# Attention values of the last steps on one Trainium2 core: two split bursts of groups 28 and 30 placed as one burst each

## The chip, the cores and the metric

The kernel runs on one core of a Trainium2 chip. The metric is the device time of one execution in microseconds (us); less is better. The kernel before takes 639.27 us, the median of three runs (638.93 to 641.06).

## The reference

For eight sequences of 512 tokens with 512 features, attention with 16 heads of 32 features is added to the input. A conditioning row is projected too and added to queries and keys, not to values.

```python
Q = split(x @ Wq.T + bq); K = split(x @ Wk.T + bk); V = split(x @ Wv.T + bv)
cQ = Q + split(tokens @ Wq.T + bq); cK = K + split(tokens @ Wk.T + bk)
scores = einsum('bhqd,bhkd->bhqk', cQ, cK) / sqrt(32)
out = einsum('bhqk,bhkd->bhqd', softmax(scores), V)
x = x + merge(out)
```

## The kernel before, in words

The work is cut into 32 groups (`G` = 8 sequences times 4 sets of four heads). A group needs, in this order: its projections; 16 *maxima* matmuls (line 429), each followed by a VectorE reduction of its bank to row maxima (line 751); 16 *scores* matmuls (line 447), each followed by a ScalarE exponential out of the bank into SBUF (line 647); three GpSimd additions over the four key chunks (line 959), for the softmax sums; the *values* matmuls (line 467), four key chunks of four heads, one head in each quarter of the output bank; the *totals* (line 475), small matmuls that finish the sums; and on VectorE the inverse of the sums, its turn, the product and the addition of bias and input (lines 784, 800, 807, 821). A matmul of values is shown as two records in the trace, so a chunk of four matmuls is "x8" there and "x4" in the program's order.

TensorE's order is written by hand. Step t has 16 slots; slot n issues scores n of group t, then as many maxima of the group ahead and projection matmuls as tables say (`MAXIMA`, `LATE_PROJ`), and at chosen slots a burst of values of group t-1. In step 29 (i = 0) and 30 (i = 1) maxima of groups 30 and 31 run; step 31 (i = 2) has only scores. The projections end in slot 3 of step 29. `END_VALUES_AT` says at which slots of the last three steps the bursts stand.

What waits for what near the change:

- A maxima matmul uses one of two banks and waits for the reduction two before it (`maxima`, wait on `v_mx`).
- A scores matmul waits for the exponential that last used its bank. There are two such banks up to slot 6 of step 29, three from slot 7 on (`END_BANKS`), and four from slot 12 of step 30 on. The fourth was a maxima bank, so scores of slot 12 of step 30 wait for all reductions of maxima (`scores`, wait on `v_mx` for `SLOTS * G`).
- A burst of values waits for its exponentials (`a_e`), and for the finished group that used its output bank (`v_f`).
- `end_totals(g)` waits for the key sums of g on VectorE (`v_s`), and for the inverse of group g-1 (`v_f`).
- The first GpSimd addition of group 29 waits for the exponentials of slots 4 to 7 of step 29 (`add`, `a_e`). GpSimd then makes five additions in a row, three for group 29 and two for group 30, and `last_sums(30)` on TensorE waits for the last (`p_a`), behind the first half of the values of group 31 in slot 11 of step 31.
- The maxima rows of group 31 go to SBUF by four small DMAs after the last reduction (line 1037), and scores of slot 0 of step 31 wait for them (`d_mr`).

The bank of a scores matmul follows from this piece, the oldest of the n banks that are open:

```python
n = 2
for i, slot, banks in END_BANKS:
    if u >= SLOTS * (G - 4 + i) + slot:
        n = banks
i = min(range(n), key=lambda i: last_use[i])
```

Of the kernel before, what the change touches and what calls it, by code (L numbers as in the profile page):

```python
# [14 lines left out]
KC = D // P  # L15
G = B * KC
# [52 lines left out]
LATE_LO = ((5, 13), (16, 24), (32, 34), (40, 47))  # L69
LATE_V = (50, 57, 67, 69)  # L70

END_VALUES_AT = ((5, 13), (15,), (3, 7))
END_TURN_AT = 5
END_SUMS_AT = 11
POOL_ADDS = 2
# [5 lines left out]
def cond_attention(nc, xT, condT, wqT, wkT, wvT, biasT, outT):  # L81
    with ExitStack() as ctx:  # L82
# [146 lines left out]
        for u in range(SLOTS * G):  # L229
# [5 lines that stand above are left out]
# [8 lines left out]
        def o_bank(g):  # L243
            return {G - 3: other_bank(), G - 2: OB[1], G - 1: OB[0]}[g] if g >= G - 3 else OB[g % 2]
# [34 lines left out]
        def maxima_at(t, n):  # L279

            return FIRST_MAXIMA[n] if t == 0 else 1 if t < G - EARLY else MAXIMA[t - (G - EARLY)][n] if t < G - 1 else 0

        def exponentials(g):
            return Pt2 if g in (G - 3, G - 1) else Pt
# [13 lines left out]
        def st_unit(g, kc, j):  # L298
            return SLOTS * g + 4 * kc + j + 1

        def finished(g, i):
            return FIN * g + i
# [17 lines left out]
        def tensor_program(e):  # L320
# [61 lines left out]
            def condition_sum(bk):  # L382
                e.wait_ge(p_sel, 5)
                e.wait_ge(a_tc, 1)
                for c in range(KC):
                    for j in range(4):
                        m = e.matmul(bk[32 * j:32 * j + 32, 32 + c * B:32 + (c + 1) * B],
                                     rr[:, c * P + 32 * j:c * P + 32 * j + 32], sel[:, 0:B], start=True, stop=True)
                m.then_inc(t_vb, 1)
# [17 lines left out]
            def project(kind, g, n):  # L407
                if kind == "v":
                    project_v(g, n)
                else:  # L410
                    project_qk("qk".index(kind), g, n)

            def maxima(u, total=None):
                g, m = divmod(u, SLOTS)
                qc, j = divmod(m, 4)
                q, k = stacked(0, g), stacked(1, g)
                if u >= 2:
                    e.wait_ge(v_mx, u - 1)
                if total is not None:
                    e.wait_ge(v_f, finished(total, 1))  # L420
                if m == 0:
                    stack_landed(e, 0, g)
                    stack_landed(e, 1, g)
                    if g < NSLOT:
                        e.wait_ge(p_ks, g + 1)
                        e.wait_ge(v_z, g + 1)
                    if g == G - 4:
                        e.wait_ge(d_ks, 48)
                e.matmul(MXB[u % 2][:, :], q[:, j, qc * P:(qc + 1) * P], k[:, j, :],  # L429
                         start=True, stop=True).then_inc(t_mx, 1)  # L430

            def scores(g, n):
                kc, j = divmod(n, 4)
                q, k = stacked(0, g), stacked(1, g)
                if n == 0:
                    e.wait_ge(d_mr[g % 2], 64 * (g // 2 + 1))
                u = SLOTS * g + n
                if st_bank_before[u] >= 0:
                    e.wait_ge(a_e, st_bank_before[u] + 1)
                elif u < 2:  # L440

                    e.wait_ge(v_lo, 3 + u)
                elif st_bank_of[u] == 2:
                    e.wait_ge(a_v, G)
                else:
                    e.wait_ge(v_mx, SLOTS * G)
                e.matmul(st_bank(u)[:, :], k[:, j, kc * P:(kc + 1) * P], q[:, j, :],  # L447
                         start=True, stop=True).then_inc(t_st, 1)

            def values(g, chunks):  # L450
                b, c = divmod(g, KC)
                if 0 in chunks:
                    if g == G - 3:
                        e.wait_ge(v_ml, 1)
                    elif g >= G - 2:
                        e.wait_ge(v_f, finished(g - 3, FIN))
                    elif g >= 2:
                        e.wait_ge(v_f, finished(g - 2, FIN))
                if g == 1 and 0 in chunks:
                    e.wait_ge(v_vb, 1)  # L460
                for kc in chunks:
                    if c == 0:
                        e.wait_ge(a_v, KC * b + kc + 1)
                    e.wait_ge(a_e, st_unit(g, kc, 3))
                    for j in range(4):
                        h = 4 * c + j
                        m = e.matmul(o_bank(g)[32 * j:32 * j + 32, :], V[:, b % 2, kc, h * HD:(h + 1) * HD],  # L467
                                     exponentials(g)[:, kc, j, :], start=(kc == 0), stop=(kc == KC - 1))
                    m.then_inc(t_pv, 1)

            def totals(g, bk):

                e.wait_ge(v_s, 2 * (g + 1))
                for j in range(4):
                    m = e.matmul(bk[32 * j:32 * j + 32, 0:16], sel[:, :], part_sums[:, g % 2, j, :],  # L475
                                 start=True, stop=True)
                m.then_inc(t_l, 1)

            def end_totals(g):

                e.wait_ge(v_mx, SLOTS * G)
                e.wait_ge(v_f, finished(g - 1, 1))
                totals(g, MXB[0])
# [43 lines left out]
            for t in range(G):  # L527
                i = t - (G - 3)
                if t < G - EARLY:
                    work = [(k, t + 3, n) for k in "vqk" for n in range(12)]  # L530
                    done = 0
                elif t == G - EARLY:
                    work = [(k, g, n) for k, g in LATE for n in range(12)]
                    done = 0
                for n in range(SLOTS):
                    scores(t, n)
                    count = 0
                    if t < G - EARLY:
                        count = (PROJ if t else FIRST_PROJ)[n]
                    elif t < G - 2:  # L540
                        count = LATE_PROJ[t - (G - EARLY)][n]
                    todo = work[done:done + count]
                    done += len(todo)
                    for m in range(maxima_at(t, n)):
                        if m > 0:
                            for k, g, p in todo[:1]:
                                project(k, g, p)
                            todo = todo[1:]
                        maxima(u, held)
                        u, held = u + 1, None  # L550
                    for k, g, p in todo:
                        project(k, g, p)
                    if i < 0 and n == VALUES_AT and t >= 1:
                        values(t - 1, range(TOTALS_BEHIND))
                        if t >= 2:
                            e.wait_ge(v_mx, u - 1)
                            totals(t - 2, MXB[u % 2])
                            held = t - 2
                        values(t - 1, range(TOTALS_BEHIND, KC))
                        if t == 1:  # L560
                            condition_sum(OB[1])
                    elif i < 0:
                        pass
                    elif i == 0 and n == END_VALUES_AT[i][0]:
                        values(t - 1, (0, 1, 2, 3) if len(END_VALUES_AT[i]) == 1 else (0, 1))
                    elif n == END_VALUES_AT[i][0]:
                        values(t - 1, (0,))
                        end_totals(t - 3)
                        values(t - 1, (1, 2, 3) if len(END_VALUES_AT[i]) == 1 else (1,))
                    elif n in END_VALUES_AT[i] and t < G - 1:  # L570
                        values(t - 1, (2, 3))
                    elif n in END_VALUES_AT[i]:
                        values(t - 1, (2,))
                        end_totals(G - 3)
                        values(t - 1, (3,))
                    if t == G - 1 and n == END_SUMS_AT:
                        values(G - 1, LAST_EARLY)
                        last_sums(G - 2, (0,) + tuple(range(POOL_ADDS + 1, KC)))
# [548 lines left out]
        @block.tensor  # L1127
        def _(e):
            tensor_program(e)
# [51 lines left out]
```

## Time and profile before

| | |
|---|---|
| median of three runs | 639.27 us |
| the profiled execution, its own time | 639.64 us |
| its span on the core | 637.8 us |
| TensorE matmul busy | 631.6 us, 99% |
| VectorE busy | 542.4 us, 85% |
| GpSimd busy | 490.2 us, 77% |
| ScalarE busy | 390.2 us, 61% |

The span is the part of an execution between its first and last recorded instruction; 1.84 us of the profiled execution lie outside it. Matmuls are pipelined, so a matmul row's duration overlaps the next one; the pace is read from the distance of starts. Times in the trace are microseconds from the span's start. PE is TensorE, PEld its weight loads, DVE VectorE, ACT ScalarE, POOL GpSimd.

### The profile page before, as it was taken

To read this page: it belongs to the slowest core of one execution; us is meant where nothing else is said; L and a number is where in the kernel's file an instruction comes from. 1 tells how busy PE (TensorE), PEld (TensorE's weight loads), DVE (VectorE), ACT (ScalarE), POOL (GpSimd) and SP (SyncE) were. 2 spreads that over 40 slices of the span, in tenths; PEclk is the share of its full clock that TensorE was granted. 3 is DMA by queue.
4 is the path that set the end of the run, shared out by engine and by line. 5 is a ranking of instruction groups with operands and counts; after the bars stand their busy time and mean duration, and the time that the engine had idled before them with its cause. 6 is when DMAs were issued, how large, how long until landed. Compare 5 with 4: busy or idle time off the path is not lost.

```text
span 637.8 us, 10063 instructions
## 1 busy us (share of the span) xinstructions
PE 631.6 (99%) x3528; PEld 441.0 (69%) x3528; DVE 542.4 (85%) x818; ACT 390.2 (61%) x684; POOL 490.2 (77%) x204
## 2 busy tenths in 40 slices
PE   8999999999999999999999999999999999999997
PEld 6777677666677666776666776666776666876642
DVE  6886888888888888888888888888888889998697
ACT  6366567666566565666665666665676655555773
POOL 6448877778877788877788777788777787767993
PEclk9999999999999999999999999999999999999999
DMA  8944435555335564434564344554354556555201
GB/s 254 272 102 119 104 103 127 121 152 145 97 102 122 138 152 126 107 105 119 149 151 116 105 115 118 151 151 106 105 126 118 151 127 158 134 120 130 76 31 67
DMA packets 48243, 80.83 MB, mean 127 GB/s; under 512 B 9545, under 2 KB 9801, under 8 KB 48073
## 3 DMA queue, kind: packets, MB, share of 16 engines
q1 hardware_dynamic: 47837, 80.04, 48.7%
q8 instruction: 28, 0.46, 0.3%
q14 instruction: 22, 0.18, 0.1%
q10 hardware_dynamic: 356, 0.16, 0.1%
HBM read 19.95 MB, written 8.39 MB: 44 GB/s over the span
## 4 chain that ended last, share of the span: by engine, by line
PE 97%; DVE 1%; DMA 1%; SPq 0%; POOLq 0%; ACT 0%; issue 0%
PE bank L354 27%; PE bank L447 19%; PE bank L429 18%; PE bank L467 18%; PE bank L402 14%; DVE bank L751 1%; PE bank L498 1%; DMA Pt<-xT 1%; PE bank L475 0%; PE bank L379 0%; DVE Xl L720 0%; POOLq L82 0%; ACT Xh L594 0%; DVE rr L789 0%; DVE rr L800 0%
## 5 line engine op out<-in xcount | busy, mean ns | idle before, releaser
L647 ACT ACTIVATE Pt<-bank 128x512 f32<-128x512 f32 x512 | 301.0, 599 | 222.1 <-PE bank L447 156.7
L751 DVE TENSOR_REDUCE mf<-bank 128x1 f32<-128x512 f32 x496 | 330.9, 684 | 60.7 <-PE bank L429 59.7
L959 POOL TENSOR_TENSOR A<-A,Pt 128x2048 f32<-128x2048 f32 x59 | 271.3, 4598 | 4.6
L429 PE MATMUL bank<-Ks,Qs 128*128 128x512 f32 x496 | 194.3, 392 | 0.1
L447 PE MATMUL bank<-Qs,Ks 128*128 128x512 f32 x496 | 194.0, 398 | 0.3 <-DVE bank L751 0.3
L959 POOL TENSOR_TENSOR A<-Pt 128x2048 f32<-128x2048 f32 x30 | 138.4, 4612 | 25.5 <-DVE part_sums L776 22.1
L447 PEld LDWEIGHTS bank<-Qs,Ks 128*128 128x128 f32 x496 | 92.6, 188 | 46.9 <-ACT Pt L647 23.3
L467 PE MATMUL bank<-Pt,V 128*32 128x512 f32 x1024 | 119.0, 596 | 0.0
L429 PEld LDWEIGHTS bank<-Ks,Qs 128*128 128x128 f32 x496 | 93.0, 188 | 21.7 <-DVE bank L751 1.8
L354 PE MATMUL bank<-Xh,Wh 128*128 128x512 f32 x256 | 100.1, 391 | 0.4 <-ACT Xh L594 0.3
L354 PE MATMUL bank<-Xl,Wh 128*128 128x512 f32 x256 | 99.8, 390 | 0.3 <-DVE Xl L720 0.3
L354 PE MATMUL bank<-Xh,Wl 128*128 128x512 f32 x256 | 99.8, 390 | 0.0
L929 POOL TENSOR_TENSOR Xl<-xr,Xh 128x512 fp32r<-128x512 f32 x28 | 36.1, 1288 | 58.7 <-ACT Xh L608 58.7
L776 DVE TRANSPOSE_TENSOR_REDUCE part_sums<-A 128x32 f32<-128x1024 f32 x58 | 71.1, 1228 | 0.0
L467 PEld LDWEIGHTS bank<-Pt,V 128*32 128x32 f32 x1024 | 26.9, 110 | 50.4 <-issue 48.9
L354 PEld LDWEIGHTS bank<-Xh,Wh 128*128 128x128 f32 x256 | 48.2, 188 | 11.3 <-ACT Wh L586 0.8
L354 PEld LDWEIGHTS bank<-Xl,Wh 128*128 128x128 f32 x256 | 48.1, 188 | 10.6 <-DVE Xl L720 0.6
L354 PEld LDWEIGHTS bank<-Xh,Wl 128*128 128x128 f32 x256 | 48.0, 188 | 10.2 <-DVE Wl L715 0.3
L402 PE MATMUL bank<-Wvh,Xh 128*128 128x512 f32 x128 | 50.2, 392 | 0.0
L402 PE MATMUL bank<-Wvh,Xl 128*128 128x512 f32 x128 | 50.1, 391 | 0.0
L402 PE MATMUL bank<-Wvl,Xh 128*128 128x512 f32 x128 | 50.0, 390 | 0.0
L739 DVE SCALAR_TENSOR_TENSOR lo<-bank,b,hi 128x512 fp32r<-128x512 f32 x62 | 46.0, 741 | 3.9 <-ACT hi L622 3.9
(74 smaller groups left out, 392.6 us busy)
## 6 DMA issues: line engine op xcount, KB each, us to landing
Qs<-hi SPq DMA_DIRECT2D x60, 256.0 KB
Ks<-hi SPq DMA_DIRECT2D x60, 256.0 KB, 4.0
Qs<-lo SPq DMA_DIRECT2D x30, 256.0 KB
Ks<-lo SPq DMA_DIRECT2D x30, 256.0 KB, 3.9
xr<-xT SPq DMA_DIRECT2D x28, 256.0 KB, 2.7
res<-xT SPq DMA_DIRECT2D x28, 256.0 KB, 2.9
outT<-ot SPq DMA_DIRECT2D x28, 256.0 KB, 3.6
Qs<-mt SPq DMA_DIRECT2D x122, 4.0 KB
```

The source lines that it names most:

```text
L354: m = e.matmul(ring_bank(use)[:, :], w[:, qk, c, kc * P:(kc + 1) * P], x[:, b % 2, kc, :], start=(n == 0), stop=(n == 11))
L402: m = e.matmul(ring_bank(use)[:, :], x[:, b % 2, kc, c * P:(c + 1) * P], w[:, kc, :], start=(n == 0), stop=(n == 11))
L429: e.matmul(MXB[u % 2][:, :], q[:, j, qc * P:(qc + 1) * P], k[:, j, :], start=True, stop=True).then_inc(t_mx, 1)
L447: e.matmul(st_bank(u)[:, :], k[:, j, kc * P:(kc + 1) * P], q[:, j, :], start=True, stop=True).then_inc(t_st, 1)
L467: m = e.matmul(o_bank(g)[32 * j:32 * j + 32, :], V[:, b % 2, kc, h * HD:(h + 1) * HD], exponentials(g)[:, kc, j, :], start=(kc == 0), stop ...
L498: m = e.matmul(sums_bank(g)[32 * j:32 * j + 32, :], ones[:, :], added_up(g)[:, j, :] if kc == 0 else exponentials(g)[:, kc, j, :], start=( ...
L647: e.activation(exponentials(g)[:, kc, j, :], st_bank(u)[:, :], ACT.Exp, scale=SCALE).then_inc(a_e, 1)
L739: e.scalar_tensor_tensor(lo_part(qk, g), ring_bank(("qk"[qk], g))[:, :], b2[:, qk, c:c + 1], hi_part(qk, g).bitcast(F32), ALU.add, ALU.sub ...
L751: e.reduce_max(to[:, 4 * j + qc:4 * j + qc + 1], MXB[u % 2][:, :], AXX).then_inc(v_mx, 1)
L776: e.tensor_reduce(part_sums[:, g % 2, 2 * i:2 * i + 2, :].rearrange("p j n -> p (j n)"), added_up(g)[:, 2 * i:2 * i + 2, :].rearrange("p j ...
L929: e.tensor_tensor(Xl[:, b % 2, kc, :], xr[:, n % 2, :], Xh[:, b % 2, kc, :].bitcast(F32), ALU.subtract).then_inc(p_x, 1)
L959: e.tensor_tensor(sums, ex[:, 0, :, :] if kc == 1 else sums, ex[:, kc, :, :], ALU.add).then_inc(p_a, 1)
```

## The change

Three bursts move; nothing is added or removed, and only TensorE's order differs. In step 29, the values of group 28 stood in two halves, chunks 0 and 1 in slot 5 and chunks 2 and 3 in slot 13; now all four stand in slot 6. Step 30 is unchanged (all values of group 29, with the totals of group 27 inside, in slot 15). In step 31, the values of group 30 stood in slot 3 (chunk 0, totals of 28, chunk 1) and slot 7 (chunk 2, totals of 29, chunk 3); now slot 5 has totals of 28, chunks 0, 1, 2, totals of 29 and chunk 3.

```diff
-END_VALUES_AT = ((5, 13), (15,), (3, 7))
+END_VALUES_AT = (6, 15, 5)
...
-                    elif i == 0 and n == END_VALUES_AT[i][0]:
-                        values(t - 1, (0, 1, 2, 3) if len(END_VALUES_AT[i]) == 1 else (0, 1))
-                    elif n == END_VALUES_AT[i][0]:
+                    elif i == 0 and n == END_VALUES_AT[i]:
+                        values(t - 1, range(KC))
+                    elif i == 1 and n == END_VALUES_AT[i]:
                         values(t - 1, (0,))
                         end_totals(t - 3)
-                        values(t - 1, (1, 2, 3) if len(END_VALUES_AT[i]) == 1 else (1,))
-                    elif n in END_VALUES_AT[i] and t < G - 1:
-                        values(t - 1, (2, 3))
-                    elif n in END_VALUES_AT[i]:
-                        values(t - 1, (2,))
-                        end_totals(G - 3)
+                        values(t - 1, (1, 2, 3))
+                    elif n == END_VALUES_AT[i]:
+                        end_totals(t - 3)
+                        values(t - 1, (0, 1, 2))
+                        end_totals(t - 2)
                         values(t - 1, (3,))
```

TensorE, step 29 from slot 4 on, the order before (L447 is scores, L429 maxima, L467 values; the first two rows are slot 4):

```order
L447 MATMUL bank<-Qs,Ks 128x512
L429 MATMUL bank<-Ks,Qs 128x512
L447 MATMUL bank<-Qs,Ks 128x512
L429 MATMUL bank<-Ks,Qs 128x512
L467 MATMUL bank<-Pt,V 32x512 x8
L447 MATMUL bank<-Qs,Ks 128x512
L429 MATMUL bank<-Ks,Qs 128x512
L447 MATMUL bank<-Qs,Ks 128x512
```

The same place in the changed kernel:

```order
L447 MATMUL bank<-Qs,Ks 128x512
L429 MATMUL bank<-Ks,Qs 128x512
L447 MATMUL bank<-Qs,Ks 128x512
L429 MATMUL bank<-Ks,Qs 128x512
L447 MATMUL bank<-Qs,Ks 128x512
L429 MATMUL bank<-Ks,Qs 128x512
L467 MATMUL bank<-Pt,V 32x512 x16
L447 MATMUL bank<-Qs,Ks 128x512
```

Scores and maxima of slot 6 now stand ahead of the burst, the burst is twice as long, and the second burst, eight slots on, is gone.

TensorE, step 31 from its slot 0 to the end of slot 11, as a piece of the difference (L475 is totals):

```order
-L447 MATMUL bank<-Qs,Ks 128x512 x4
-L467 MATMUL bank<-Pt,V 32x512 x4
-L475 MATMUL bank<-part_sums,sel 32x16 x4
-L467 MATMUL bank<-Pt,V 32x512 x4
-L447 MATMUL bank<-Qs,Ks 128x512 x4
-L467 MATMUL bank<-Pt,V 32x512 x4
-L475 MATMUL bank<-part_sums,sel 32x16 x4
-L467 MATMUL bank<-Pt,V 32x512 x4
-L447 MATMUL bank<-Qs,Ks 128x512 x4
+L447 MATMUL bank<-Qs,Ks 128x512 x6
+L475 MATMUL bank<-part_sums,sel 32x16 x4
+L467 MATMUL bank<-Pt,V 32x512 x12
+L475 MATMUL bank<-part_sums,sel 32x16 x4
+L467 MATMUL bank<-Pt,V 32x512 x4
+L447 MATMUL bank<-Qs,Ks 128x512 x6
```

Three runs of four scores with two short bursts between them have become two runs of six with one long burst between them.

## Rows read from the trace of the kernel before

**Rows 1.** The page: busy time by engine, and TensorE's granted clock in 40 slices.

```profile
PE 631.6 (99%) x3528; PEld 441.0 (69%) x3528; DVE 542.4 (85%) x818; ACT 390.2 (61%) x684; POOL 490.2 (77%) x204
PEclk9999999999999999999999999999999999999999
```

**Rows 2.** Chain that ended last, 594 to 638: start us, us, what.

```profile
606.65 3.98 DVE bank L751 x6
...
610.63 2.00 DVE bank L751 x3
```

**Rows 3.** Timeline of PE, step 29: start us, us, what [idle before].

```profile
598.37 1.92 PE L467 MATMUL bank<-Pt,V 128*32 128x512 f32 x16
600.22 0.50 PE L447 MATMUL bank<-Qs,Ks 128*128 128x512 f32 x1
...
603.45 0.41 PE L447 MATMUL bank<-Qs,Ks 128*128 128x512 f32 x1
603.79 1.92 PE L467 MATMUL bank<-Pt,V 128*32 128x512 f32 x16
605.65 0.72 PE L447 MATMUL bank<-Qs,Ks 128*128 128x512 f32 x2
606.21 0.40 PE L429 MATMUL bank<-Ks,Qs 128*128 128x512 f32 x1
606.45 0.40 PE L447 MATMUL bank<-Qs,Ks 128*128 128x512 f32 x1
```

**Rows 4.** Timeline of PE, end of step 30 and step 31.

```profile
612.67 1.20 PE L447 MATMUL bank<-Qs,Ks 128*128 128x512 f32 x4 [0.33 <-DVE bank L751]
613.80 1.07 PE L467 MATMUL bank<-Pt,V 128*32 128x512 f32 x8
...
614.74 2.76 PE L467 MATMUL bank<-Pt,V 128*32 128x512 f32 x24
617.43 1.19 PE L447 MATMUL bank<-Qs,Ks 128*128 128x512 f32 x4
618.56 1.06 PE L467 MATMUL bank<-Pt,V 128*32 128x512 f32 x8
...
620.48 1.21 PE L447 MATMUL bank<-Qs,Ks 128*128 128x512 f32 x4
...
624.68 1.92 PE L467 MATMUL bank<-Pt,V 128*32 128x512 f32 x16
626.42 1.04 PE L498 MATMUL bank<-A,ones 128*32 128x512 f32 x8
```

**Rows 5.** Timeline of DVE, row maxima of group 31 in step 29.

```profile
598.11 1.30 DVE L751 TENSOR_REDUCE bank<-bank 128x1 f32<-128x512 f32 x2 [0.31 <-PE bank L429]
...
600.99 3.36 DVE L751 TENSOR_REDUCE bank<-bank 128x1 f32<-128x512 f32 x5 [1.47 <-PE bank L429]
```

**Rows 6.** Timeline of ACT, steps 28 to 31.

```profile
589.76 0.60 ACT L647 ACTIVATE Pt<-bank 128x512 f32<-128x512 f32 x1 [0.15 <-PE bank L447]
...
598.81 0.63 ACT L630 ACTIVATE V<-bank 128x512 f32<-128x512 f32 x1
600.76 4.03 ACT L647 ACTIVATE Pt<-bank 128x512 f32<-128x512 f32 x8 [1.32 <-PE bank L447]
606.18 9.18 ACT L647 ACTIVATE Pt<-bank 128x512 f32<-128x512 f32 x18 [1.40 <-PE bank L447]
618.05 2.06 ACT L647 ACTIVATE Pt<-bank 128x512 f32<-128x512 f32 x4 [2.69 <-PE bank L447]
```

**Rows 7.** Timeline of PEld in step 29: a weight load that waited for an exponential.

```profile
606.83 0.19 PEld L447 LDWEIGHTS bank<-Qs,Ks 128*128 128x128 f32 x1 [0.19 <-ACT Pt L647]
```

**Rows 8.** Timeline of POOL: additions of groups 28 to 30, first and last.

```profile
598.51 4.59 POOL L959 TENSOR_TENSOR V<-V,Pt 128x2048 f32<-128x2048 f32 x1 [0.15 <-issue]
603.05 4.61 POOL L959 TENSOR_TENSOR A<-Pt 128x2048 f32<-128x2048 f32 x1
...
621.65 4.59 POOL L959 TENSOR_TENSOR A<-A,Pt 128x2048 f32<-128x2048 f32 x1
```

## The prediction, made before the changed kernel ran

> **What bounds the kernel now.** I read the page first, then the chain of waits, then the timeline of each engine over the last 45 us, since the change touches nothing ahead of slot 6 of step 29 (598.3 us in the trace). The page says that TensorE is busy 99% of the span, at full granted clock in every slice [rows 1], so for most of the kernel the time is the sum of matmuls. The reader should not carry that figure into the last steps. The chain of waits shows there the one long stretch that is not TensorE: nine VectorE reductions of row maxima back to back, 606.65 to 612.63 [rows 2], ended by scores of slot 12 of step 30, which start at 612.67 after a wait for that last reduction [rows 4]. Behind it TensorE is the chain again, with short trips over its neighbours. So two questions decide: does the last reduction end earlier or later, and does TensorE need more or less time from there to the end?
>
> **Prices, from the rows.** In a plain run, starts of 128-wide matmuls lie 0.23 to 0.24 apart (606.21 and 606.45 [rows 3]). A chunk of values takes 0.86: three chunks from 614.74 to 617.43 are 2.69, of which about 0.11 to 0.14 is the way back to scores [rows 4]. A burst also costs at its edges: from scores at 603.45 to maxima at 606.21 are 2.76 us, where three plain distances (0.69) and two chunks (1.72) make 2.41; so 0.35 us for one burst [rows 3] (0.11 on the way in, 0.14 on the way out, 0.11 behind the first matmul). An exponential starts 0.53 us behind the start of its scores after a burst (605.65 to 606.18 [rows 3, 6]), in step 31 0.62 (617.43 to 618.05 [rows 4, 6]); in a row they come every 0.51 (9.18 us for 18 [rows 6]). The bank is free for TensorE 0.65 behind the start of the exponential (606.18 to the weight load at 606.83 [rows 6, 7]), and the matmul follows 0.07 later. A reduction takes 0.66 (5.98 for nine [rows 2]) and starts 0.44 behind its maxima (606.21 to 606.65 [rows 3, 2]).
>
> **The change part by part.**
>
> *Fewer bursts.* Two bursts fewer on TensorE, one in step 29 and one in step 31: 2 x 0.35 = 0.7 us less matmul path, if nothing else were to wait. The number of chunks and totals is the same. The Trainium skill (TensorEngine Tiling (Array Packing), Key Properties) says that changing the tiling mode drains TensorE, which speaks for fewer changes of mode and by itself for a gain; by that rule alone the sum would be 0.7 us less. The weighing below is what speaks against it.
>
> *Step 29, the single burst of four chunks.* Scores and maxima of slot 6 now come ahead of the burst. These maxima are the third of group 31 and need the bank of the first, whose reduction begins at 598.11 [rows 5] and ends at 598.8. So the burst begins at about 599.1 in place of 598.37 [rows 3]; four chunks and the way out are 3.44 + 0.14, and scores of slot 7 start at 602.7. Their exponential starts at 603.2. Before it, ScalarE had been idle only for 1.32 and 1.40 us around the two bursts [rows 6]; now it has nothing from about 600 to 603.2, as the two banks hold no more than two scores. From slot 7 on three banks are open, so scores of slot 15 wait for exponential 12, the sixth after the burst: it starts at 603.2 + 5 x 0.51 = 605.8, and frees the bank for a matmul at 605.8 + 0.72 = 606.5. Maxima of slot 15 follow 0.34 later, their reduction 0.44 behind them: 607.3, where the row before says 606.65. From this one on there are nine reductions (this, and eight in step 30) as before, with VectorE the slower partner: they end at 607.3 + 5.97 = 613.3 in place of 612.63. **Term A: +0.65 us.** The burst saved lies in that figure: it is used up, since after one long gap VectorE and ScalarE have each lost more than after two short ones, during which two full banks bridged the gap twice. Step 30's burst and the maxima rows by DMA hang on the last reduction and shift with it: from 612.67 to 617.43 everything is as before [rows 4]. The DMAs themselves are the same, and neither SP nor ScalarE has another job issued past them.
>
> *Step 31, six scores in a row.* Four banks are open there. Before, each run had four scores and never met a full bank: from the first scores at 617.43 to the values of group 31 at 624.68 were 7.25 us [rows 4]. Now the fifth scores of a run wait for the first exponential. Counted from the first scores of the run: exponential 0 starts at 0.62, frees its bank at 1.34; scores 4 could have gone at 0.34 + 3 x 0.23 = 1.03, so they wait 0.3. Exponential 1 frees its bank at 1.85, so scores 5 go at 1.85, and the burst begins at 2.19. Without waits it would have begun at 1.6. So each run of six costs 0.58 us more, and there are two: +1.16, less the one burst's edges saved, 0.35: **term B: +0.8 us.** In the burst the totals of 28 and of 29 stand behind work of VectorE that is done by then: key sums of 28 end more than 4 us ahead; the inverse of 28 is ready at about 621.1, and totals of 29 come at about 622.9. If one of these were late, all values behind it would be too; I price it at nothing, because of these 2 us and more. VectorE's own chain (finishing 27 to 29, then an addition of 3.1 us) moves with term A, and is needed by TensorE only after slot 15.
>
> *GpSimd.* Its first addition of group 29 starts at 603.05 right behind the one of group 28, and five in a row end at 621.65 + 4.59 = 626.24 [rows 8]; TensorE takes the sum at 626.42 [rows 4]. So there is hardly any slack: shortening TensorE's path before this place can gain 0.1 to 0.2 us at most. Now the first of these additions waits for exponential 7, which ends at 603.2 + 0.51 = 603.7; with 0.1 for the hand-over it starts at 603.8, 0.75 later than before, and the last ends at 627.0. TensorE arrives with terms A and B at 626.42 + 1.45 = 627.9, so I cost this delay at nothing: it is covered by terms A and B, and is what the time falls back to (+0.7 us) if they are smaller.
>
> *The end.* From slot 12 of step 31 on (last scores, last sums, values, finishing) the rows depend on TensorE alone, and move with it.
>
> **Sum:** 0.65 + 0.8 = 1.45; I take +1.4 us, since the second of two waiting scores may recover some hundredths. Against the profiled execution of 639.64 us that is 641.0. The median of the three runs shown, 639.27, lies 0.37 below that execution, so the median of the changed kernel is forecast at **640.7 us**. The bounds: term A could be 0.4 (the exponential after the burst starts some tenths earlier) to 1.2 (exponentials 0.60 apart, the duration of a lone one [rows 6], over five of them, adds 0.45). Term B could be 0.3 (the waits hidden by half) to 1.2 (0.60 apart, two per run, with one more hand-over). A measurement of this kernel tells about 0.3%, 1.9 us, from no change.
>
> **The rivals.**
>
> 1. *GpSimd's chain decides.* Terms A and B are smaller than I think, and the last sums wait for the addition: +0.7 us, 640.0. For it speaks the slack of 0.1 to 0.2 us before [rows 4, 8]; against it, two waits on full banks that I can't see vanish.
> 2. *Slower by more than 0.3%: the exponentials run at 0.60 and not 0.51.* In step 28, where ScalarE is fed one bank at a time, it takes 0.60 and stands idle 0.15 more [rows 6]. If the stretch behind the long burst is fed so, slot 15 comes 5 x 0.09 = 0.45 later (A = 1.1), and the four waiting scores of step 31 cost 0.09 or 0.15 more each (B = 1.2): +2.3 us, 641.6. It decides where the distance exceeds about 0.56. Against it stand 18 exponentials in a row at 0.51 with three and four banks [rows 6].
> 3. *Only the edges of the bursts count.* No wait of A or B reaches the end, and the 0.7 us saved on TensorE stay: 638.6. The rule on changes of tiling mode would have it so. Against it is GpSimd's chain, which allows at best 0.2 us while its first addition starts no later.
> 4. *The change does something else than it says.* The order on TensorE shows exactly these moves and nothing on other engines, so I leave this nearly no chance.
>
> **How the numbers follow.** Forecast (A and B as priced, 639.9 to 641.2): 0.57. Rival 1: 0.18. Rival 2, and other ways over 1.9 us slower: 0.20. Rival 3, 0.04, and rival 4, 0.01. The range from 639.5 to 642.0 takes in the forecast with its bounds, rival 1 with the scatter of a median, and rival 2. Faster by over 0.3% needs 1.9 us, more than twice what the bursts' edges can give: 0.02. Slower by over 0.3% is rival 2 and a forecast that meets a high median: 0.22. The rest, 0.76, is within 0.3%.
>
> **What would show it.** In the profile after: values x32 in one row from 599.1 to 602.6; ScalarE idle over 3 us before 603.2, then some 25 exponentials without a gap; VectorE's last run of reductions starting at about 607.3 and ending at 613.3; scores of slot 12 of step 30 still released by it; in step 31 two weight loads in each run of six that wait for an exponential; last sums of group 30 at 627.9, with GpSimd done at 627.0; everything behind it moved by the same 1.4 us. I would be wrong if the last reduction ended before 612.7, if the runs of six took under 1.8 us, or if the last sums were released by GpSimd.

## The result, and the profile after

The changed kernel takes **640.7 us**, the median of 20 runs (640.03 to 642.44), against 639.32 (638.76 to 641.06, 20 runs) for the kernel before: a ratio of 1.0022, 95% interval 1.0016 to 1.0027. It is 1.4 us slower, less than the 0.3% that the prediction counts as a difference, but its interval does not reach 1, so the loss is real. The profiled execution took 640.79 us, its span 639.0.

A few disturbed executions of the experiments below ran at a fraction of the clock or far longer; the ratios leave them out, and the first trace of the joined step 29 (904.4 us at a granted clock of 0.656) is not used.

**A common start.** The code ahead of the change is the same in all kernels here, but the time from the span's start to the first reduction of group 31 is not: 598.11 us before [rows 5], 597.88 after, and from 597.20 to 598.39 over the experiments. A quarter of a microsecond is about a sixth of this result. So below every time of a trace is counted from that reduction, as "x from the start". The last run of reductions then begins at 606.65 - 598.11 = 8.54 before.

Timeline of VectorE after, the reductions of group 31 (columns as in [rows 5]):

```profile
597.88 1.30 DVE L750 TENSOR_REDUCE bank<-bank 128x1 f32<-128x512 f32 x2 [0.31 <-PE bank L429]
...
599.21 0.66 DVE L750 TENSOR_REDUCE bank<-bank 128x1 f32<-128x512 f32 x1
603.39 2.00 DVE L750 TENSOR_REDUCE bank<-bank 128x1 f32<-128x512 f32 x3 [3.53 <-PE bank L429]
605.56 0.70 DVE L750 TENSOR_REDUCE bank<-bank 128x1 f32<-128x512 f32 x1 [0.17 <-PE bank L429]
607.03 5.97 DVE L750 TENSOR_REDUCE bank<-bank 128x1 f32<-128x512 f32 x9 [0.77 <-PE bank L429]
```

Line numbers in the changed kernel are one less than before; those of the experiments differ from either by up to two. Three reductions, then VectorE has nothing for 3.53 us, and two more gaps of 0.17 and 0.77 before the last nine begin at 9.15 from the start: 0.61 later than before. Before there were gaps of 1.47 [rows 5] and 2.29 us, and five reductions between them (timeline of VectorE before):

```profile
606.65 5.97 DVE L751 TENSOR_REDUCE bank<-bank 128x1 f32<-128x512 f32 x9 [2.29 <-PE bank L429]
```

Timeline of ScalarE after:

```profile
599.04 0.65 ACT L646 ACTIVATE Pt<-bank 128x512 f32<-128x512 f32 x1
603.16 12.58 ACT L646 ACTIVATE Pt<-bank 128x512 f32<-128x512 f32 x25 [3.47 <-PE bank L447]
618.42 3.05 ACT L646 ACTIVATE Pt<-bank 128x512 f32<-128x512 f32 x6 [2.68 <-PE bank L447]
624.23 3.04 ACT L646 ACTIVATE Pt<-bank 128x512 f32<-128x512 f32 x6 [2.76 <-PE bank L447]
```

One idle stretch of 3.47 us, then 25 exponentials without a gap, 0.50 us each. In step 31, two runs of six.

Timeline of TensorE after, the burst of step 29, then from the end of step 30 to the last sums (to be read beside [rows 3, 4]):

```profile
599.05 3.64 PE L467 MATMUL bank<-Pt,V 128*32 128x512 f32 x32
602.63 0.50 PE L447 MATMUL bank<-Qs,Ks 128*128 128x512 f32 x1
...
613.05 1.19 PE L447 MATMUL bank<-Qs,Ks 128*128 128x512 f32 x4 [0.33 <-DVE bank L750]
...
617.81 2.26 PE L447 MATMUL bank<-Qs,Ks 128*128 128x512 f32 x6
620.00 0.26 PE L475 MATMUL bank<-part_sums,sel 128*32 128x16 f32 x8
620.08 2.76 PE L467 MATMUL bank<-Pt,V 128*32 128x512 f32 x24
...
623.69 2.17 PE L447 MATMUL bank<-Qs,Ks 128*128 128x512 f32 x6
625.79 1.92 PE L467 MATMUL bank<-Pt,V 128*32 128x512 f32 x16
627.53 1.04 PE L498 MATMUL bank<-A,ones 128*32 128x512 f32 x8
```

Scores of slot 12 of step 30 are still released by the last reduction. From the first scores of step 31 to the values of group 31 are 7.98 us, where [rows 4] give 7.25. The last sums begin at 627.53 - 597.88 = 29.65 from the start, before at 28.31: 1.34 later.

Timeline of the weight loads of the first run of six:

```profile
617.80 0.77 PEld L447 LDWEIGHTS bank<-Qs,Ks 128*128 128x128 f32 x4 [0.84 <-DMA Qs<-mt]
619.07 0.19 PEld L447 LDWEIGHTS bank<-Qs,Ks 128*128 128x128 f32 x1 [0.50 <-ACT Pt L646]
619.56 0.19 PEld L447 LDWEIGHTS bank<-Qs,Ks 128*128 128x128 f32 x1 [0.30 <-ACT Pt L646]
```

Four loads go through, the fifth and the sixth wait for an exponential, as term B has it. The loads begin 619.07 - 618.42 = 0.65 after exponential 0 did: the price read from step 29 holds here. The 0.84 with the name of a DMA is the gap that every way out of a burst shows; whether the small DMAs landed last by a hair is not told apart, and it is the same before.

Timeline of GpSimd after, the first and the last of the five additions:

```profile
603.90 4.60 POOL L958 TENSOR_TENSOR A<-Pt 128x2048 f32<-128x2048 f32 x1 [1.10 <-ACT Pt L646]
...
622.47 4.59 POOL L958 TENSOR_TENSOR A<-A,Pt 128x2048 f32<-128x2048 f32 x1
```

The first addition waits for exponential 7, as foretold, but starts at 6.02 from the start, not 4.94 as before: 1.08 late, where I had 0.75. The last ends at 29.18, still 0.47 ahead of the last sums, so the delay stays hidden, with less to spare than the 0.9 that I had worked out. Where TensorE does stand before this addition (`s29_again` and `s29_slot5` below), the sums begin 0.15 behind its end. So of these 0.47 us 0.32 were to spare, and of the 0.18 between 28.13 and 28.31 in the kernel before only 0.03.

### The profile page after: what moved, and what is told of

Same layout as the page of the kernel before. It is cut to its first block, busy times and chain, and to the rows that moved or that the text cites. A ratio compares the mean times of both kernels' runs of the same rounds, so it can differ in the third digit from the quotient of the medians.

```text
span 639.0 us, 10063 instructions
## 1 busy us (share of the span) xinstructions
PE 632.9 (99%) x3528; PEld 440.7 (69%) x3528; DVE 543.1 (85%) x818; ACT 390.0 (61%) x684; POOL 490.3 (77%) x204
## 4 chain that ended last, share of the span: by engine, by line
PE 97%; DVE 1%; DMA 0%; ACT 0%; POOLq 0%; issue 0%; ACTq 0%; DVEq 0%
PE bank L354 27%; PE bank L447 19%; PE bank L429 18%; PE bank L467 18%; PE bank L402 14%; DVE bank L750 1%; PE bank L498 1%; DMA cond<-condT 0%; ACT Pt L646 0%; PE bank L475 0%; PE bank L379 0%; DVE Xl L719 0%; POOLq L82 0%; ACT Xh L593 0%; DVE rr L788 0%; DVE rr L799 0%
## 5 line engine op out<-in xcount | busy, mean ns | idle before, releaser
L447 PE MATMUL bank<-Qs,Ks 128*128 128x512 f32 x496 | 195.3, 399 | 0.5 <-DVE bank L750 0.3
L429 PE MATMUL bank<-Ks,Qs 128*128 128x512 f32 x496 | 194.3, 392 | 0.0
L447 PEld LDWEIGHTS bank<-Qs,Ks 128*128 128x128 f32 x496 | 92.7, 188 | 47.9 <-ACT Pt L646 23.7
L467 PE MATMUL bank<-Pt,V 128*32 128x512 f32 x1024 | 118.5, 596 | 0.0
L429 PEld LDWEIGHTS bank<-Ks,Qs 128*128 128x128 f32 x496 | 93.0, 188 | 21.4 <-DVE bank L750 1.7
L467 PEld LDWEIGHTS bank<-Pt,V 128*32 128x32 f32 x1024 | 27.2, 110 | 51.0 <-issue 48.9
```

## The experiments

The theory: term A (VectorE and ScalarE run empty behind one long burst in step 29) and term B (six scores meet four banks in step 31) add up, and GpSimd's delay lies under them. The rivals: only the bursts' edges count; GpSimd's chain alone decides; or the long burst itself, or a totals matmul in it, costs the time. Where a trace decides, its figures stand in this table; all are differences of two starts, in us:

| kernel | last nine reductions begin | GpSimd's last addition ends | last sums begin | last values begin | median against before |
|---|---|---|---|---|---|
| before | 8.54 | 28.13 | 28.31 | 33.88 | |
| changed | 9.15 | 29.18 | 29.65 | 35.23 | +1.38 |
| both_again | 9.17 | 29.17 | 29.69 | 35.24 | +1.19 |
| s29_again | 9.16 | 29.19 | 29.34 | 34.92 | +0.92 |
| s31_only | 8.53 | 28.09 | 29.03 | 34.58 | +0.71 |
| s29_slot5 | 8.72 | 28.77 | 28.92 | 34.49 | +0.61 |
| bank3_late | 10.27 | 29.17 | 30.80 | 36.35 | +2.38 |

### One join at a time

`s29_only` and its repetition `s29_again` join step 29 alone:

```diff
-END_VALUES_AT = ((5, 13), (15,), (3, 7))
+END_VALUES_AT = ((6,), (15,), (3, 7))
```

> Only step 29's bursts are joined (slot 6); step 31 stays as before. My theory (term A: VectorE's last nine reductions begin later, because ScalarE and VectorE stand empty behind one long burst): the last reduction ends 0.6 later than before against the common start of the trace, the stretch from the first scores of step 31 to the values of group 31 stays at 7.25 us, the whole is +0.6 to +0.7 us, and GpSimd's last addition ends within 0.2 us of TensorE's need of it. Rival, that the edges of the bursts count: -0.35 us. Rival, that GpSimd's chain alone decides: the last reduction does not move, and the end still does, by 0.7.

> The kernel of s29_only again, since the profile of its first run shows a granted clock of 0.656 and cannot be laid beside the others, and its median came out 0.6 us higher than I expected. My theory: in the trace, counted from the first reduction of group 31, the last nine reductions begin 0.6 later than before and the last sums of group 30 1.2 to 1.3 earlier than the changed kernel's plus 0.6, that is 0.6 to 0.7 later than before; the whole +0.6 to +0.8. If the two joins don't add (the rival): the trace shows another 0.5 us in step 31 or at its end.

Measured: 640.39 against 639.12 us for the first (ratio 1.0016, 1.0007 to 1.0025), 640.29 against 639.37 for the second (1.0015, 1.0006 to 1.0024). The medians are 1.27 and 0.92 us higher, both above what was expected; their intervals are a microsecond wide and take in the 1.03 that the trace shows. In the trace of the second the last nine reductions begin 0.62 later, as expected. But the last sums begin 1.03 later, not 0.6 to 0.7, and the row says why (timeline of TensorE, `s29_again`):

```profile
624.51 1.92 PE L467 MATMUL bank<-Pt,V 128*32 128x512 f32 x16
626.69 1.07 PE L498 MATMUL bank<-A,ones 128*32 128x512 f32 x8 [0.26 <-POOL A L959]
```

TensorE stands before GpSimd's last addition. Term A on TensorE's path is right (624.51 is 27.16 from the start, 0.59 more than the 26.57 before), but alone it is not the price of this join: GpSimd's chain is, rival 1, in a place where I had left it only the fall-back. The expectation missed by 0.4 us for one reason, the 1.08 of GpSimd's first addition. The stretch from the first scores of step 31 to the values is unchanged (7.2), so the joins do not disturb each other there.

`s31_only` joins step 31 alone (the edit is shown against the changed kernel):

```diff
-END_VALUES_AT = (6, 15, 5)
+END_VALUES_AT = ((5, 13), 15, 5)
...
-                    elif i == 0 and n == END_VALUES_AT[i]:
-                        values(t - 1, range(KC))
+                    elif i == 0 and n in END_VALUES_AT[i]:
+                        values(t - 1, (0, 1) if n == END_VALUES_AT[i][0] else (2, 3))
```

> Only step 31's bursts are joined (slot 5); step 29 stays as before. My theory (term B: two runs of six scores over four banks wait for exponentials): 7.25 us becomes 8.0, nothing else moves, the whole is +0.7 to +0.8 us. Rival, edges only: -0.35 us on TensorE, at most 0.1 to 0.2 of it in the end. Rival, a totals matmul that waits for VectorE inside the long burst: the burst of 16 values records and totals takes over 3.8 us.

Measured: 639.83 against 639.12 us (ratio 1.0007, 0.9998 to 1.0016). The interval takes in no change; the trace is sharper: the last nine reductions begin where they did (8.53), and 7.25 became 7.99, from 616.80 to 624.79. The burst with both totals took the same 3.7 us as in the changed kernel (618.98 to 622.68), so no totals matmul waited:

```profile
616.80 2.25 PE L447 MATMUL bank<-Qs,Ks 128*128 128x512 f32 x6
618.98 0.26 PE L475 MATMUL bank<-part_sums,sel 128*32 128x16 f32 x8
...
622.68 2.17 PE L447 MATMUL bank<-Qs,Ks 128*128 128x512 f32 x6
624.79 1.92 PE L467 MATMUL bank<-Pt,V 128*32 128x512 f32 x16
```

`both_again` is the changed kernel once more, on the chip of `s29_again`.

> The changed kernel again on the chip of the two single joins. If terms A and B add: +1.3 to +1.5 us, the sum of the single joins by their traces (0.6 + 0.7).

Measured: 640.56 against 639.37 us (ratio 1.0023, 1.0013 to 1.0032), and by the trace the last sums come 1.38 late. The single joins give 1.03 + 0.72 = 1.75 by the traces. They do not add, and the rows say what is shared: 0.4 us of the first is a wait for GpSimd, and with the second TensorE arrives after GpSimd has ended. On TensorE's path alone they add: 0.6 + 0.7.

### The place of the burst

`s29_slot5` puts all values of group 28 in slot 5 (`((5,), (15,), (3, 7))`).

> Step 29's values all in slot 5 and not 6, step 31 as before. Tells the burst's place from its length. My theory: the burst starts 0.7 us earlier than in slot 6, so the last reduction ends only 0.3 to 0.4 later than before; but exponential 7 still comes 0.6 late, so GpSimd's chain is now what the last sums wait for, and the end is +0.5 to +0.6, not +0.35. If GpSimd's chain did not matter: +0.35. If the place did not matter: +0.65, as with slot 6.

Measured: 639.73 against 639.12 us (ratio 1.0006, 0.9996 to 1.0015, which takes in 1; the readings are of the trace). The last nine begin 0.18 later (I had 0.3 to 0.4), and the last sums 0.61 later, released by GpSimd:

```profile
626.54 1.07 PE L498 MATMUL bank<-A,ones 128*32 128x512 f32 x8 [0.24 <-POOL A L959]
```

So the place matters as much as the length. The weight loads of slot 6 say why. In the changed kernel they stand ahead of the burst, and both wait:

```profile
598.27 0.19 PEld L447 LDWEIGHTS bank<-Qs,Ks 128*128 128x128 f32 x1 [0.47 <-ACT Pt L646]
598.63 0.19 PEld L429 LDWEIGHTS bank<-Ks,Qs 128*128 128x128 f32 x1 [0.17 <-DVE bank L750]
```

The scores wait for an exponential (their bank is one of two), the third maxima of group 31 for the first reduction. One slot earlier neither stands ahead of the burst: it begins 0.25 from the start (597.87) and not 1.17, 0.9 earlier where I had 0.7, and of term A only 0.2 us is left. What the end loses beyond that is the wait for GpSimd.

### Banks and exponentials

`half31_before` and `half31_after` leave out half of the columns of the exponentials of slots 0 to 11 of step 31, in `exps`:

```diff
-                e.activation(exponentials(g)[:, kc, j, :], st_bank(u)[:, :], ACT.Exp, scale=SCALE).then_inc(a_e, 1)
+                w = HALF if g == G - 1 and n < 12 else S
+                e.activation(exponentials(g)[:, kc, j, 0:w], st_bank(u)[:, 0:w], ACT.Exp, scale=SCALE).then_inc(a_e, 1)
```

> Left out: exponentials of slots 0 to 11 of step 31 write only half of their columns, so each takes about 0.3 us and not 0.5; order as before. All theories: nothing waits for these exponentials in the order before, so 7.25 us from the first scores of step 31 to the values of group 31 stay as they are (7.2 to 7.3).

> The same work left out (half of the columns of the exponentials of slots 0 to 11 of step 31), in the changed order. My theory of term B (the fifth and sixth scores of a run wait for exponentials, and nothing else): with a short exponential the waits vanish, and the stretch becomes 7.25 - 0.35 = 6.9 us, shorter than before, where the full exponentials made 8.0. If the long burst itself, its totals or VectorE cost the time, it stays near 8.0. The last sums of group 30 then wait for GpSimd.

Measured in one execution each (timeline of TensorE, first the order before, then the changed order):

```profile
616.96 1.19 PE L447 MATMUL bank<-Qs,Ks 128*128 128x512 f32 x4
...
624.19 1.92 PE L467 MATMUL bank<-Pt,V 128*32 128x512 f32 x16
```

```profile
618.34 1.83 PE L447 MATMUL bank<-Qs,Ks 128*128 128x512 f32 x6
620.10 0.26 PE L475 MATMUL bank<-part_sums,sel 128*32 128x16 f32 x8
...
625.47 1.92 PE L467 MATMUL bank<-Pt,V 128*32 128x512 f32 x16
627.72 1.07 PE L498 MATMUL bank<-A,ones 128*32 128x512 f32 x8 [0.32 <-POOL A L959]
```

The order before keeps its 7.23 us. The changed order falls from 7.98 to 7.13, and is now the shorter one. I had 6.9: the first run of six still takes 1.76 and the second 1.67 (623.80 to 625.47), not 1.6, since a half exponential lasts 0.38 us and, with the 0.62 ahead of it, leaves a short wait. The sign has turned, and with it the rivals that blame the burst or its totals fall. Of these 0.85 us the end gains only 0.33 (the last values begin 34.90 from the start, not 35.23), because the last sums then wait for GpSimd, as expected.

`bank3_late` is the changed kernel with the third bank opened nine slots later:

```diff
-END_BANKS = ((1, 7, 3), (2, 12, 4))
+END_BANKS = ((1, 16, 3), (2, 12, 4))
```

> The changed order, but the third bank of scores opens only at slot 0 of step 30 and not at slot 7 of step 29. Tests whether banks and exponentials set the pace of TensorE behind the long burst of step 29. My theory: with two banks scores of slots 8 to 15 of step 29 come about 0.6 us apart and not 0.5, the last nine reductions begin 0.9 to 1.0 us later than in the changed kernel, and the whole is about +2.3 us on the kernel before (+0.9 on the changed one). If the pace there were set by VectorE or by TensorE's own work: no change against the changed kernel.

Measured: 641.84 against 639.46 us (ratio 1.0039, 1.0028 to 1.005). The last nine reductions begin 1.12 later than in the changed kernel (I had 0.9 to 1.0), the last sums 1.15 and the last values 1.12. Behind the long burst the exponentials of slots 7 to 13 start 0.59 apart, as foretold, where the changed kernel has 0.48. So there it is banks times exponentials that sets TensorE's pace.

`s29_maxima` is `s29_again` with the maxima of step 29 placed more densely behind the long burst:

```diff
-          (1, 0, 1, 1, 1, 1, 1, 1, 0, 1, 1, 0, 1, 0, 0, 1),
+          (1, 0, 1, 1, 1, 1, 0, 0, 1, 1, 0, 1, 1, 1, 0, 1),
```

> The single burst in slot 6 of step 29, with the maxima of group 31 placed densely behind it (slots 8, 9, 11, 12, 13, 15 in place of 6, 7, 9, 10, 12, 15), step 31 as before. Tests that term A is VectorE running out of maxima behind the long burst: the gap ahead of its last run of reductions closes, and the last reduction ends 0.4 us earlier than in the joined kernel, 0.2 to 0.3 later than before. GpSimd's first addition of group 29 still comes 0.5 late, so the last sums are released by GpSimd and the whole is +0.4 to +0.5 us. If TensorE's own work set term A: no change against s29_again.

Measured: 639.97 against 639.37 us (ratio 1.0006, 0.9997 to 1.0015, which takes in 1). Timeline of VectorE, and the last sums on TensorE:

```profile
598.17 1.30 DVE L751 TENSOR_REDUCE bank<-bank 128x1 f32<-128x512 f32 x2 [0.31 <-PE bank L429]
603.57 9.40 DVE L751 TENSOR_REDUCE bank<-bank 128x1 f32<-128x512 f32 x14 [3.99 <-PE bank L429]
```

```profile
627.14 1.07 PE L498 MATMUL bank<-A,ones 128*32 128x512 f32 x8 [0.19 <-POOL A L959]
```

Fourteen reductions without a gap end at 14.80 from the start; in `s29_again` the last ended at 15.14, before at 14.51. So 0.34 of term A's 0.62 comes back, and a wait for GpSimd is left, as expected. The gaps of 0.17 and 0.77 are filled, but that is not the whole of the edit: slot 6 has no maxima now, so the burst begins 0.36 earlier (0.82 from the start, 1.18 in `s29_again`), the first reduction behind it 0.12 earlier (5.40, not 5.52), and one reduction of 0.66 more stands behind it. VectorE then has no gap left, so its gaps were part of term A; how the 0.34 divides between them and the earlier burst, this run does not tell. The rest (+0.66 at the last sums) was 0.2 above what I wrote, again by GpSimd's start (5.67 from the start).

### The other direction

`split3_late` and its repetition `split3_again` use three bursts in step 29 and move the last sums of group 30 behind the last scores:

```diff
-END_VALUES_AT = ((5, 13), (15,), (3, 7))
+END_VALUES_AT = ((5, 9, 13), (15,), (3, 7))
...
-                    elif i == 0 and n == END_VALUES_AT[i][0]:
-                        values(t - 1, (0, 1, 2, 3) if len(END_VALUES_AT[i]) == 1 else (0, 1))
+                    elif i == 0:
+                        if n in END_VALUES_AT[0]:
+                            values(t - 1, ((0,), (1,), (2, 3))[END_VALUES_AT[0].index(n)])
...
                         values(G - 1, LAST_EARLY)
-                        last_sums(G - 2, (0,) + tuple(range(POOL_ADDS + 1, KC)))
+            last_sums(G - 2, (0,) + tuple(range(POOL_ADDS + 1, KC)))
             last_sums(G - 1, LAST_ORDER)
```

> The other direction: step 29's values in three bursts (chunk 0 in slot 5, chunk 1 in slot 9, chunks 2 and 3 in slot 13), one burst's edges more on TensorE (+0.35), and the last sums of group 30 behind slots 12 to 15 of step 31, so that GpSimd's last addition is no floor. My theory: VectorE and ScalarE starve less, the last reduction ends 0.1 to 0.2 earlier, the whole is -0.1 to -0.2 us. If only edges counted: +0.35.

> The kernel of split3_late again: its trace, counted from the first reduction of group 31, ends only 0.1 us later than before, but its median was 1.0 us higher. If the order of the last steps is the cause, the median comes down to +0.1 to +0.3; if it stays at +1.0, something ahead of step 29 differs between the programs, that the order does not name.

Measured: 640.15 against 639.12 us (ratio 1.0016, 1.0007 to 1.0025), then 640.01 against 639.37 (1.0013, 1.0004 to 1.0022). I missed both times. The last nine begin 0.1 later, not earlier. And "something ahead of step 29" was the wrong guess for the rest: it lies behind the last values, where I had not looked. Timeline of VectorE in `split3_again`, and in the kernel before:

```profile
628.84 0.72 DVE L790 STREAM_TRANSPOSE rr<-bank 128x512 f32<-128x512 f32 x1 [1.32 <-PE bank L498]
...
631.36 0.75 DVE L822 SCALAR_TENSOR_TENSOR ends<-bank,vb,lo 128x512 f32<-128x512 f32 x1
632.21 0.72 DVE L790 STREAM_TRANSPOSE rr<-bank 128x512 f32<-128x512 f32 x1
...
634.80 0.48 DVE L836 SCALAR_TENSOR_TENSOR ends<-bank,vb,lo 128x256 f32<-128x256 f32 x1
```

```profile
632.24 0.72 DVE L789 STREAM_TRANSPOSE rr<-bank 128x512 f32<-128x512 f32 x1 [0.58 <-PE bank L498]
...
634.83 0.48 DVE L835 SCALAR_TENSOR_TENSOR ends<-bank,vb,lo 128x256 f32<-128x256 f32 x1
```

Before, VectorE has finished group 30 and waits 0.58 us for the last sums of group 31. With the sums of 30 moved back it waits 1.32 us for those first, and then finishes 30 and 31 without a pause. Its last instruction starts 634.80 - 597.24 = 37.56 from the start, before 36.72 (634.83 - 598.11): 0.84 us later, between the two medians' 1.03 and 0.64. So the slack of GpSimd was bought with one on VectorE that is only 0.58 wide.

### An addition fewer on GpSimd

`pool_adds1` is the kernel before with `POOL_ADDS = 1`.

> The order before, with one addition of group 30 fewer on GpSimd and one chunk more of last sums on TensorE. Two things: the chunk costs 0.86 us on TensorE and is on the path, +0.8 to +0.9 us. And VectorE's addition of group 31 (3.10 us before, 3.66 in the changed kernel) no longer runs beside a GpSimd addition: if the two hold each other up, it takes 2.1 to 2.2 us now; if its duration has another cause, it stays at 3.1 or more.

Measured: 639.94 against 639.46 us (ratio 1.0006, 0.9993 to 1.0019); in the trace the last values begin 34.70 from the start, 0.82 later, as one chunk costs. The median is only 0.48 higher, with an interval that takes in no change as well as the 0.82. What VectorE's addition did is told in the last section. No version here beats the kernel before.

## Why the prediction was right

The median came out at the predicted 640.7 us. By its own steps:

- *Term A, +0.65:* 0.61 in the trace (0.62 and 0.63 in the repetitions), from the start of the last nine reductions. The single steps fit too. The burst starts 1.17 from the start, at 599.3 of the clock of before, for the 599.1 foretold; scores of slot 7 and exponential 7 come 0.2 later than foretold each (4.75 and 5.28 from the start, foretold 4.6 and 5.1). Most of that comes back because exponentials 7 to 12 start 0.48 apart and not 0.51 (603.16 to 605.56; the mean of all 25 is 0.50), and scores of slot 15 are then released by exponential 12, as foretold, 0.70 behind its start (605.56). Timeline of the weight loads:

```profile
606.26 0.19 PEld L447 LDWEIGHTS bank<-Qs,Ks 128*128 128x128 f32 x1 [0.30 <-ACT Pt L646]
```

That banks and exponentials set the pace is shown by these waits and by `bank3_late`; that VectorE's gaps are part of the term, by `s29_maxima`.

- *Term B, +0.8:* 0.73. Two waits per run, on the fifth and sixth scores, with the release at 0.65. The first run takes 2.19 (617.81 to 620.00), as worked out, the second 2.10. Its cause is shown by the half exponentials. The totals inside the burst were priced at nothing because of "2 us and more"; the prediction's own two times are 1.8 apart, and the inverse of 28 was ready at 620.74, 1.5 ahead of the totals of 29 (weight load at 622.23). They did not wait.
- *The edges of a burst, 0.35:* they were not measured alone. An estimate from the half exponentials: that order is 0.10 shorter (7.23 less 7.13) although its two runs of six take 0.23 more than the 1.6 each worked out for a run without waits, which makes 0.33 for one burst.
- *GpSimd, costed at nothing:* right for the changed kernel, where 0.47 us were left. But the term was mis-sized: 1.08 late, not 0.75. Exponential 7 started 0.2 later than foretold, and the addition 0.14 behind its end, where I had 0.1. And the prediction let it last 0.51, which is the distance of starts in a row; taken alone it lasts from 603.16 to 603.76, 0.60. In both traces of step 29 joined alone, in slot 6 or in slot 5, this chain is what the end waits for. Had term B been under 0.4, rival 1 would have been the result, at +1.0 and not the +0.7 that I gave it.
- *The sum:* 0.61 + 0.73 = 1.34, and 1.34 was found at the last sums; the median says 1.38.
- *Rival 2* (exponentials 0.60 apart) didn't happen: 25 in a row took 12.58 us. *Rival 3*, the edges alone, fell: two bursts fewer, and the kernel is slower. With it fell what the prediction drew from the Trainium skill's rule on changes of the tiling mode (TensorEngine Tiling (Array Packing), Key Properties), taken as the whole account; nothing in the runs speaks against the rule itself.

That the figure met the median to a tenth owes something to luck: the prediction leaned on a median of three, and the terms missed by 0.04 and 0.07 in the same direction. Inside term A two misses of near 0.2 cancelled, the later burst and the denser exponentials.

## What to carry to other kernels

Joining two bursts saves their edges (here some 0.35 us, an estimate), but the engines that are fed between them must live from full banks during the whole of it, and two short bursts let the same banks bridge twice. Count the banks against the length of the run that follows as well: with four banks here four scores went through, and the fifth waited for the whole round through ScalarE. Before an order near the end is changed, write down every neighbour's slack at the point where TensorE takes its result; here these were 0.03 us on GpSimd and 0.58 us on VectorE, and they decided which saving or loss counted, so that losses of single edits did not add.

## What was not expected of the hardware

VectorE's addition of group 31 (a tensor of 2048 columns from two others, all in SBUF) took 3.10 us before and 3.66 after, with the same work. It is the time that it runs beside GpSimd's last addition that differs. Timeline of VectorE before, in the changed kernel, in `bank3_late` and in `pool_adds1`:

```profile
625.28 3.10 DVE L796 TENSOR_TENSOR V<-Pt 128x2048 f32<-128x2048 f32 x1
```

```profile
625.55 3.66 DVE L795 TENSOR_TENSOR V<-Pt 128x2048 f32<-128x2048 f32 x1
```

```profile
626.00 2.54 DVE L795 TENSOR_TENSOR V<-Pt 128x2048 f32<-128x2048 f32 x1
```

```profile
624.64 2.28 DVE L796 TENSOR_TENSOR V<-Pt 128x2048 f32<-128x2048 f32 x1
```

GpSimd's addition ended 0.96 us behind the start of the first, 1.51 behind that of the second, 0.37 behind that of the third, and 3.7 ahead of the fourth. Duration less overlap is 2.14, 2.15, 2.17 and 2.28, and it stays between 2.14 and 2.17 in all twelve traces with an overlap. So VectorE's instruction makes next to no headway until GpSimd's has ended, and then needs 2.15 us; why it takes 0.13 more when it runs alone, no run shows. The Trainium skill (SBUF — State Buffer, Who interferes with whom) says the same: a VectorE instruction with two SBUF inputs contends with a GpSimd instruction that reads SBUF, and whichever comes second blocks until the first has finished. The traces agree for this pair, where GpSimd's addition came first; the other order was not tried. It cost nothing here, since TensorE takes the sum only after slot 15 (the addition ends at 629.21 in the changed kernel, the matmul starts at 630.51), but the end of this addition is tied to the end of GpSimd's, not to its own start, and must be counted so.
